# Moving the 8-bit coding of x and context from ScalarE to VectorE, and attention's row term from the front to the down stage

## The chip, the cores and the metric

The kernel runs on one NeuronCore of a Trainium2 chip. The core has TensorE (PE, matrix products into PSUM), VectorE (DVE), ScalarE (ACT), GpSimd (POOL) and SyncE (SP), which here issues nearly every DMA, in one queue and in program order. Every engine works through its own instructions in order and waits for others by semaphores. The metric is the device time of one execution in microseconds (us).

## The reference, cut to what matters

`x` is (2, 512, 1024), the context (2, 1024, 1024), both float32. The block is a quantised product with the context, then a quantised gated feed-forward layer (hidden width 2752):

```
q1 = fake_quant(layernorm(x), s1, z1)      # clip(round(v / s + z), 0, 255), minus z, times s
q2 = fake_quant(ctx, s2, z2)
x1 = x + tanh(g_xattn) * (q1 @ q2)
A  = blockwise fp8 of layernorm(x1), the last 128 columns twice (value and remainder)
h  = silu(A @ Wg.T * g) * (A @ Wu.T * g)   # Wg, Wu: blockwise int4
out = x1 + tanh(g_ffn) * (blockwise fp8 of h) @ Wd.T * gm
```

With zero points that are not whole numbers, q1 @ q2 has, beside the product of whole-number codes, a term for each column and a term for each row. The row term is one number per row of x. It cancels in the layernorm of x1, so the kernel adds it apart from the rest, to the copy of x1 that goes into the output.

## The kernel before, in words

The 1024 rows of x are 8 tiles of 128 (t = 0..7), the 2048 context rows 16 tiles (c = 0..15). Everything is written out by hand, engine by engine: the order in the source is the order on the engine, and there is no scheduler.

**Front (about 0 to 83 us).** SP loads x (`load_x`), then context tiles (`load_ctx`) into six buffers, so load c waits until code c - 6 is made (semaphore `ctx_affine`). Weight pieces for the first products (`load_piece(0)` to `(3)`) are loaded in between. Context tile c goes through `relu_ctx(c)` on ACT (scale, add the zero point, clip below at 0, write uint8 with rounding and saturation into one of two byte buffers `ctx_int`), `shift_ctx(c)` on POOL (subtract the rounded zero point, write bf16 into `ctxq`), and `col_sums` on PE. Tile t of x goes through `first_stats(t)` on DVE, `layernorm` (one call for tiles 0 to 3, one for 4 to 7), `relu_x(t)` on ACT (as for the context), `quantise_x(t)` on DVE (uint8 to bf16), `turn_x(t)` on PE (eight transposes) and `aT_out(t)` on ACT. Then PE runs `attend(t)`, and DVE's `make_x1(t)` adds the result into x. Between its first steps DVE also works out two flags (are the column permutations the identity?); SP reads them (`flags_ready`, two register loads) after `load_ctx(6)` and before `load_ctx(7)`.

**Preparation of the feed-forward layer (about 60 to 140 us).** ACT squares x1 (`square_x1`) and normalises it (`norm(t)`, `xn_done`), DVE takes block maxima (`max_a`); after all 8 tiles the maximum goes over PE (`spread_max`) and gives the global scale. From there on the activations are quantised, transposed by DMA (`turn_a`) and multiplied. In parallel, weight piece n passes DVE (`front_open`: block maxima, scales), POOL (`scale`), ACT (`round_w`, `whole_w`), POOL (`back_open`), ACT (`hi_open`), POOL (`lo_open`, `nat_lo`), and a DMA transpose (`turn_piece(n)`). `base(t)` on ACT adds the row term to x1 in place, after `norm(t)`, and SP's `store_x1(t)` puts the result to DRAM (`x1_d`). The transposed pieces 0 to 2 (`p_ring`) take the place of x1's tiles 0 to 2, so `turn_piece(0)` waits until these three tiles are stored (`x1_gone`). SP's order here is load_piece(4), store_x1(0), store_x1(1), load_piece(5), store_x1(2), turn_piece(0), load_piece(6), store_x1(3) and so on; load_piece(n) waits for lo_open(n - 4).

**Main loop and down stage (140 us to the end).** PE runs gate and up products and, from 589 us, the down products, 130 matmuls for each row tile. In the down stage ACT makes `magic_h` and `hi_h` for each half of a row tile, DVE the rest of the quantisation, SP loads x1 back (`load_x1`), and DVE's `finish(t)` adds x1 to the product before `store_out(t)`.

Of the kernel before, what the change touches and what calls it, by code (L numbers as in the profile page):

```python
# [13 lines left out]
ALU = mybir.AluOpType  # L14
ACT = mybir.ActivationFunctionType
# [51 lines left out]
def gated_block(nc, x, ctx_in, g_xattn, g_ffn, s1, z1, s2, z2, w_gate, w_up, w_down, ri_in, ri_mid, out):  # L67
# [4 lines left out]
    with ExitStack() as ctx:  # L72
# [143 lines left out]
        att_done = sem("att_done")  # L216
        x_base = sem("x_base")
        x1_ready = sem("x1_ready")
# [125 lines left out]
        def _(sp):  # L344
# [495 lines left out]
        def _(act):  # L840
# [10 lines left out]

            def relu_ctx(c):

                w = ctx_buf[c % CTX_BUFS]
                act.wait_ge(ctx_loaded[c % CTX_BUFS], 16 * (c // CTX_BUFS) + 16)
                if c >= 2:

                    act.wait_ge(ctx_quant, c - 1)
                act.activation(ctx_int[:, c % 2, :], w, ACT.Relu, bias=prm[:, 3:4], scale=pinv[:, 1:2]).then_inc(ctx_affine, 1)  # L859

            def relu_x(t):

                act.wait_ge(ln_ready, t // 4 + 1)
                if t >= 2:

                    act.wait_ge(a_quant, t - 1)
                act.activation(x_int[:, t % 2, :], x_all[:, t, :], ACT.Relu, bias=ln_add[:, t:t + 1],
                               scale=ln_mul[:, t:t + 1]).then_inc(x_affine, 1)

            def aT_out(t):  # L870
# [22 lines left out]
            def norm(t):  # L893

                if t == 0:
# [5 lines left out]
                               scale=ln_mul[:, t:t + 1]).then_inc(xn_done, 1)  # L901

            def base(t):

                act.wait_ge(row_term_ready, 1)
                act.wait_ge(xn_done, t + 1)
                act.activation(x_all[:, t, :], x_all[:, t, :], ACT.Identity, bias=row_term[:, t:t + 1]).then_inc(x_base, 1)

# [79 lines left out]
            relu_x(3)
            relu_ctx(15)
            square_x1(0)  # L990
            aT_out(2)
            square_x1(1)
            relu_x(4)
            relu_x(5)
            relu_x(6)
            aT_out(3)
# [3 lines left out]
            square_x1(2)  # L1000
            relu_x(7)
            round_w(0, 1)
# [16 lines left out]
            norm(3)  # L1019
            base(0)  # L1020
            hi_open(1)
            base(1)
            hi_open(2)
            square_x1(7)
            base(2)
            round_w(3, 0)
            root(4, slice(4, NT))
            base(3)
            whole_w(3)
            norm(4)  # L1030
            round_w(4, 1)
            base(4)
            norm(5)
            hi_open(3)
            norm(6)
            base(5)
            norm(7)
            base(6)
            round_w(5, 2)
            base(7)  # L1040
            round_w(6, 3)
# [103 lines left out]
            def hi_h(n):  # L1145
# [209 lines left out]
        def _(dve):  # L1355
# [233 lines left out]
            step(dve.tensor_tensor(tt[:, 1:2], tt[:, 0:1], fz[:, 1:2], ALU.mult))  # L1589
            dve.tensor_scalar(tt[:, 2:3], tt[:, 1:2], fz[:, 0:1], float(H), ALU.mult, ALU.mult).then_inc(prm_ready, 1)  # L1590
            step(first_stats(3))
            first_stats(4)
            first_stats(5)
            dve.wait_ge(idx_loaded, 32)
# [6 lines left out]
            dve.tensor_reduce(nfl[0:64, 1:2], neq[0:64, 8:8 + nm], AX_X, ALU.max).then_inc(flag_step, 1)  # L1601
            aggregate(slice(0, 4))
            dve.wait_ge(flag_step, 5)
            dve.tensor_reduce(nall[:, 0:1], acc[3][:, 0:2 * P], AX_X, ALU.max)
            step(dve.tensor_reduce(nall[:, 1:2], acc[3][:, P:2 * P], AX_X, ALU.max))
            dve.tensor_copy(flag[:], nall[:]).then_inc(flags_ready, 1)
            layernorm(1, slice(0, 4), tt[:, 5:6], prm[:, 1:2])
            first_stats(6)
            step(first_stats(7))
            aggregate(slice(4, NT))  # L1610
            quantise_x(0)
            dve.wait_ge(flags_ready, 1)
            in_moved = dve.value_load(flag[0:1, 0:1], min_val=0, max_val=1)
            quantise_x(1)
            col_lo(0)
            quantise_x(2)
            make_x1(0)
            layernorm(2, slice(4, NT), tt[:, 5:6], prm[:, 1:2])
            make_x1(1)
            quantise_x(3)  # L1620
            quantise_x(4)
            make_x1(2)
            quantise_x(5)
            col_lo(1)
# [256 lines left out]
```

## Time and profile before

| what | us |
|---|---|
| median of 3 runs | 818.23 (816.87 to 818.39) |
| profiled execution, its own time | 818.77 |
| its span, first to last instruction | 817.0 |
| PE busy in the span | 731.0 (89%) |
| DVE busy | 556.3 (68%) |
| POOL busy | 343.7 (42%) |
| ACT busy | 311.3 (38%) |

Outside the span lie 1.77 us of the profiled execution. Busy time is a sum over stages that have different limits, so the sections below read it stage by stage. In rows of the timeline an entry with "x2" or more is several instructions in one row, and the duration is from the first start to the last end. An instruction's duration includes time in which it has started and is held up.

### The profile page before, as it was taken

What the parts mean: (1) busy time and instruction counts of PE and PEld (TensorE: products, weight loads), DVE (VectorE), ACT (ScalarE), POOL (GpSimd) and SP (SyncE); (2) the same over time, 40 slices, a digit from 0 to 9 for tenths busy, and PEclk for the clock granted to TensorE, in tenths of its full rate; (3) what the DMA queues carried; (4) which work ended last, traced back from release to release, by engine and by line L of the source; (5) the groups of instructions that cost most, each with busy time, mean ns of one, the idle gap of its engine ahead of it and who ended that gap; (6) DMA issues with size and microseconds to landing.
All of it is one profiled execution on the core that took longest, in us unless ns stands there. A gap on an engine that the chain in (4) does not pass through costs nothing.

```text
span 817.0 us, 10350 instructions
## 1 busy us (share of the span) xinstructions
PE 731.0 (89%) x3473; PEld 334.5 (41%) x3473; DVE 556.3 (68%) x957; ACT 311.3 (38%) x382; POOL 343.7 (42%) x206
## 2 busy tenths in 40 slices
PE   0599003999999999999999999999999999999998
PEld 0144002545444444444444444444444444444443
DVE  5459789894475756675757575745898888988800
ACT  2798972445252524343434343430222122121100
POOL 1536766769374747584848575740000000000000
PEclk9989655999999999999999999999999999999999
DMA  8910598339588897979697969774265654555320
GB/s 308 353 60 14 166 279 147 80 64 190 145 173 212 187 211 174 223 169 227 145 232 163 231 163 236 157 157 164 49 152 162 182 129 149 132 161 121 88 60 26
DMA packets 228884, 131.56 MB, mean 161 GB/s; under 512 B 201712, under 2 KB 212976, under 8 KB 227824
## 3 DMA queue, kind: packets, MB, share of 16 engines
q1 hardware_dynamic: 228848, 131.12, 65.2%
q8 instruction: 18, 0.29, 0.2%
q14 instruction: 18, 0.15, 0.1%
HBM read 61.88 MB, written 19.66 MB: 100 GB/s over the span
## 4 chain that ended last, share of the span: by engine, by line
PE 78%; DVE 5%; POOL 5%; DMA 5%; ACT 3%; SPq 2%; issue 1%; DVEq 0%
PE acc L1276 47%; PE acc L1330 27%; DMA big<-in_ctx_dram 3%; PE acc L1223 2%; POOL big L739 1%; POOL h_in L734 1%; DVE big L1535 1%; ACT wbuf_all L919 1%; POOL wbuf_all L715 1%; POOL wbuf_all L708 1%; POOL big L728 1%; DMA wbuf_all<-in_L_ffn_w_up_dram 1%; SPq L455 1%; DMA mid<-big 1%; DMA x_d<-big 1%
## 5 line engine op out<-in xcount | busy, mean ns | idle before, releaser
L1276 PE MATMUL acc<-mid 128*128 128x512 f16 x1920 | 415.1, 379 | 0.0
L1276 PEld LDWEIGHTS acc<-mid 128*128 128x128 f16 x1920 | 187.9, 98 | 226.1
L1330 PE MATMUL acc<-big,mid 128*128 128x512 f16 x1040 | 224.6, 379 | 0.0
L818 POOL TENSOR_TENSOR h_in<-wbuf_all,h_in 128x1024 f16<-128x1024 f32 (+1 forms) x56 | 114.4, 2044 | 97.2 <-ACT h_in L1115 97.1
L1330 PEld LDWEIGHTS acc<-big,mid 128*128 128x128 f16 x1040 | 101.8, 98 | 122.7
L708 POOL TENSOR_TENSOR wbuf_all<-wbuf_all,w_inv 128x1024 f32<-128x1024 f32 (+1 forms) x67 | 125.2, 1873 | 43.6 <-DVE w_inv L1448 43.6
L1558 DVE SCALAR_TENSOR_TENSOR h_out<-acc,gs,silu 128x256 f32<-128x256 f32 (+1 forms) x88 | 41.5, 471 | 102.6 <-ACT silu L956 65.3
L1442 DVE TENSOR_REDUCE tb<-wbuf_all 128x64 f32<-128x1024 f32 (+1 forms) x67 | 78.9, 1178 | 47.3 <-DMA wbuf_all<-in_L_ffn_w_gate_dram 22.2
L912 ACT ACTIVATE wbuf_all<-wbuf_all 128x1024 f32<-128x1024 f32 (+1 forms) x67 | 68.1, 1016 | 82.2 <-POOL wbuf_all L708 81.4
L1115 ACT ACTIVATE h_in<-wbuf_all 128x1024 f16<-128x1024 f32 (+1 forms) x56 | 56.9, 1016 | 103.1 <-DVE wbuf_all L1454 103.1
L1454 DVE SCALAR_TENSOR_TENSOR wbuf_all<-wbuf_all,tb 128x1024 f32<-128x1024 f32 (+1 forms) x56 | 65.1, 1163 | 0.3 <-issue 0.2
L1153 ACT ACTIVATE wbuf_all<-h_in 128x1408 f16<-128x1408 f32 x16 | 22.0, 1377 | 108.4 <-DVE h_in L1509 67.9
L956 ACT ACTIVATE silu<-acc,gs 128x256 f32<-128x256 f32 (+1 forms) x88 | 40.0, 456 | 50.2 <-PE acc L1276 49.4
L1143 ACT ACTIVATE wbuf_all<-h_in 128x1408 f32<-128x1408 f32 (+1 forms) x16 | 21.6, 1351 | 50.6 <-DVE h_in L1773 50.6
L1276 PE MATMUL acc<-big,mid 128*128 128x384 f16 x192 | 34.4, 341 | 2.1 <-DMA mid<-big 1.3
L1811 DVE SCALAR_TENSOR_TENSOR mid<-acc,hr,mid 128x512 f32<-128x512 f32 x16 | 11.4, 745 | 36.2 <-PE acc L1330 36.2
L1563 DVE TENSOR_REDUCE hm<-h_out 128x256 f32 (+2 forms) x88 | 34.0, 387 | 2.7
L1783 DVE SCALAR_TENSOR_TENSOR h_in<-wbuf_all,h_in 128x1408 f32<-128x1408 f32 (+1 forms) x16 | 25.4, 1587 | 10.1 <-ACT wbuf_all L1143 10.1
L1448 DVE RECIPROCAL w_inv<-tb 128x64 f32<-128x64 f32 (+1 forms) x56 | 30.2, 539 | 1.9
L1223 PE MATMUL acc<-mid,big 128*128 128x512 bf16 x128 | 31.5, 403 | 0.0
L702 POOL TENSOR_SCALAR mid<-big,nrz 128x1024 bf16<-128x1024 uint8 x16 | 18.4, 1151 | 30.4 <-ACT big L859 30.1
L1773 DVE SCALAR_TENSOR_TENSOR h_in<-mid,hr,h_in 128x1408 f32<-128x1408 f32 (+1 forms) x16 | 26.3, 1646 | 0.3
(159 smaller groups left out, 555.0 us busy)
## 6 DMA issues: line engine op xcount, KB each, us to landing
h_in<-h_d SPq DMA_DIRECT2D x8, 1376.0 KB, 7.0
wbuf_all<-in_L_ffn_w_gate_dram SPq DMA_DIRECT2D x21, 512.0 KB, 4.3
wbuf_all<-in_L_ffn_w_up_dram SPq DMA_DIRECT2D x21, 512.0 KB, 4.3
h_d<-h_out SPq DMA_DIRECT2D x80, 128.0 KB, 3.5
big<-in_ctx_dram SPq DMA_DIRECT2D x16, 512.0 KB, 10.7
wbuf_all<-in_L_ffn_w_down_dram SPq DMA_DIRECT2D x16, 512.0 KB, 4.5
big<-in_x_dram SPq DMA_DIRECT2D x8, 512.0 KB, 6.9
x_d<-big SPq DMA_DIRECT2D x8, 512.0 KB, 4.8
```

Of the source, the lines that this page charges most:

```text
L708: pool.tensor_tensor(w, w, spread(w_inv[0:rows, b, 0:cols // BLK]), ALU.mult).then_inc(w_scaled, 1)
L818: last = pool.tensor_tensor(nat[s % 4][:, H:H + cols], wbuf[:, s % 4, 0:cols], nat[s % 4][:, 0:cols], ALU.subtract)
L912: act.activation(wbuf[0:rows, b, 0:cols], wbuf[0:rows, b, 0:cols], ACT.Copy, bias=MAGIC, scale=W_UP)\
L956: act.activation(silu[:, m % 2, 0:cols], acc[m % 4][:, 0:cols], ACT.Silu, scale=gs[:, 2:3]).then_inc(silu_done, 1)
L1115: act.activation(nat[s % 4][:, 0:cols], wbuf[:, s % 4, 0:cols], ACT.Copy).then_inc(nat_hi, 1)
L1223: pe.matmul(acc[pair(t) + hf][:], aT[:, k, t * P:(t + 1) * P], ctxq[:, b * KT + k, hf * MW:(hf + 1) * MW], start=(k == 0), stop=False)
L1276: last = pe.matmul(acc[m % 4][:, 0:cols], left[:, k, s * P:(s + 1) * P], w[:, right, k, 0:cols], start=(k == 0 and left is a_hi and right ...
L1330: last = pe.matmul(acc[2 * i + hf][:], left[:, k - ks.start, :], right[:, k, hf * MW:(hf + 1) * MW], start=(k == 0 and left is hi and righ ...
L1442: dve.tensor_reduce(top, blocks(wbuf[0:rows, b, 0:cols]), AX_X, ALU.max, apply_absolute_value=True).then_inc(scale_step, 1)
L1454: dve.scalar_tensor_tensor(out=w, in0=w, scalar=MAGIC, in1=spread(block_scale(b, looped)[0:rows, 0:cols // BLK]), op0=ALU.subtract, op1=AL ...
L1558: dve.scalar_tensor_tensor(out=h_out[:, m % 2, 0:cols], in0=acc[m % 4][:, cols:2 * cols], scalar=gs[:, 2:3], in1=silu[:, m % 2, 0:cols], o ...
L1563: dve.tensor_reduce(hm[:, s, bass.ds(at, cols // BLK)], blocks(h_out[:, m % 2, 0:cols]), AX_X, ALU.max, apply_absolute_value=True).then_in ...
```

## The change

Coding of x and context is done on DVE by new functions `code_ctx` and `code_x`: one two-step tensor_scalar (multiply, add) from float32 to uint8, without the Relu, since the conversion saturates at 0. They stand in DVE's program among the first steps. ACT's 16 `relu_ctx` and 8 `relu_x` are gone, and so are its 8 `base` calls in the preparation. SP stores x1 as soon as `make_x1(t)` has made it. `turn_piece(0)` now also waits for the first three `norm` calls, which read what it overwrites. In the down stage ACT adds the row term to the x1 tile that was loaded back, in place, and `finish(t)` waits for that (`x1_based`) in place of the load.

```
+                        sp.wait_ge(xn_done, X1_FIRST)          # in turn_piece(0)
...
             def store_x1(t):
-                sp.wait_ge(x_base, t + 1)
+                sp.wait_ge(x1_ready, t + 1)
...
+            def base(t):                                       # ACT, down stage
+                i = t % 2
+                act.wait_ge(x1_loaded[i], 16 * (t // 2 + 1))
+                act.activation(x1_t[:, i, :], x1_t[:, i, :], ACT.Identity, bias=row_term[:, t:t + 1]).then_inc(x1_based, 1)
...
             magic_h(4)
+            base(0)
             for n in range(4, 2 * NT):
                 hi_h(n)
                 if n + 1 < 2 * NT:
                     magic_h(n + 1)
+                    if n % 2 == 1:
+                        base((n - 3) // 2)
+            base(NT - 2)
+            base(NT - 1)
...
+            def code_ctx(c):                                   # DVE
+                dve.wait_ge(ctx_loaded[c % CTX_BUFS], 16 * (c // CTX_BUFS) + 16)
+                if c >= 2:
+                    dve.wait_ge(ctx_quant, c - 1)
+                dve.tensor_scalar(ctx_int[:, c % 2, :], ctx_buf[c % CTX_BUFS], pinv[:, 1:2], prm[:, 3:4], ALU.mult, ALU.add)\
+                    .then_inc(ctx_affine, 1)
+            def code_x(t):
+                if t % 4 == 0:
+                    dve.wait_ge(ln_ready, t // 4 + 1)
+                dve.tensor_scalar(x_int[:, t % 2, :], x_all[:, t, :], ln_mul[:, t:t + 1], ln_add[:, t:t + 1], ALU.mult, ALU.add)\
+                    .then_inc(x_affine, 1)
...
             def finish(t):
-                dve.wait_ge(x1_loaded[i], 16 * (t // 2 + 1))
+                dve.wait_ge(x1_based, t + 1)
```

DVE's program from the parameters on is now: code_ctx(0), stats(3), code_ctx(1), first half of the flags, aggregate(0..3), code_ctx(2), second half of the flags, code_ctx(3), layernorm(1), code_ctx(4), code_x(0), stats(4), code_ctx(5), quantise_x(0), stats(5), code_ctx(6), stats(6), code_ctx(7), code_x(1), stats(7), code_ctx(8), quantise_x(1), aggregate(4..7), code_ctx(9), code_x(2), code_ctx(10), quantise_x(2), col_lo(0), code_ctx(11), code_x(3), layernorm(2), code_ctx(12), quantise_x(3), make_x1(0), code_ctx(13), code_x(4), code_ctx(14), quantise_x(4), code_ctx(15), make_x1(1), code_x(5), code_x(6), make_x1(2), quantise_x(5), col_lo(1), front_open(0), quantise_x(6), code_x(7), make_x1(3), and from there as before.

**DVE around the flags.** These rows of DVE's program run from the statistics of x's tile 3 to the end of the flag work; nfl, nall and flag are the flags, mv and ve the variance of tiles 0 to 3. Before:

```order
L1367 BN_STATS bst<-big 128x6 x6
L1597 TENSOR_TENSOR neq<-idx,iot 128x8
L1598 TENSOR_TENSOR neq<-idx,iot 64x43
L1600 TENSOR_REDUCE nfl<-neq 128x1
L1601 TENSOR_REDUCE nfl<-neq 64x1
L1372 BN_AGGR mv<-bst 128x2 x4
L1374 TENSOR_SCALAR ve<-mv 128x4
L1604 TENSOR_REDUCE nall<-acc3 128x1
L1605 TENSOR_REDUCE nall<-acc3 128x1
L1606 CAST flag<-nall 128x2
```

And these are the rows of the changed program, from the same point on (rows `big<-big,pinv,prm` are code_ctx(0), (1) and (2)):

```order
L1364 TENSOR_SCALAR big<-big,pinv,prm 128x1024
L1324 BN_STATS bst<-big 128x6 x2
L1364 TENSOR_SCALAR big<-big,pinv,prm 128x1024
L1570 TENSOR_TENSOR neq<-idx,iot 128x8
L1571 TENSOR_TENSOR neq<-idx,iot 64x43
L1573 TENSOR_REDUCE nfl<-neq 128x1
L1574 TENSOR_REDUCE nfl<-neq 64x1
L1329 BN_AGGR mv<-bst 128x2 x4
L1331 TENSOR_SCALAR ve<-mv 128x4
L1364 TENSOR_SCALAR big<-big,pinv,prm 128x1024
L1578 TENSOR_REDUCE nall<-acc3 128x1
L1579 TENSOR_REDUCE nall<-acc3 128x1
```

The last flag step (CAST) is the next row. Three codes of the context now stand ahead of it, the first of them ahead of everything.

**DVE at the first weight piece.** The rows go from the first weight piece's maxima and scales (front_open(0), w_max and w_inv) over quantise_x(6) to make_x1(3). Before:

```order
L1442 TENSOR_REDUCE tb3<-wbuf_all 128x64
L1445 TENSOR_SCALAR w_max<-tb3 128x64
L1448 RECIPROCAL w_inv<-w_max 128x64
L1407 TENSOR_SCALAR silu<-big,nrz 128x1024
L1414 SCALAR_TENSOR_TENSOR big,x_sum<-acc0,tt,big 128x512
L1414 SCALAR_TENSOR_TENSOR big,x_sum<-acc1,tt,big 128x512
```

And the same place of the changed program:

```order
L1415 TENSOR_REDUCE tb3<-wbuf_all 128x64
L1418 TENSOR_SCALAR w_max<-tb3 128x64
L1421 RECIPROCAL w_inv<-w_max 128x64
L1380 TENSOR_SCALAR silu<-big,nrz 128x1024
L1371 TENSOR_SCALAR big<-big,ln_mul,ln_add 128x1024
L1387 SCALAR_TENSOR_TENSOR big,x_sum<-acc0,tt,big 128x512
L1387 SCALAR_TENSOR_TENSOR big,x_sum<-acc1,tt,big 128x512
```

One row is new, code_x(7), between quantise_x(6) and make_x1(3).

**ACT in the preparation.** The rows go from norm(3) (`big<-big,ln_add,ln_mul`) to square_x1(7) (`hm,x_sq`) and the next round_w; `h_in<-wbuf_all` is hi_open(1) and (2). Before:

```order
L900 ACTIVATE big<-big,ln_add,ln_mul 128x1024
L907 ACTIVATE big<-big,row_term 128x1024
L928 ACTIVATE h_in<-wbuf_all 128x1024
L907 ACTIVATE big<-big,row_term 128x1024
L928 ACTIVATE h_in<-wbuf_all 128x1024
L890 ACTIVATE hm,x_sq<-big,n_mean 128x1024
L907 ACTIVATE big<-big,row_term 128x1024
L912 ACTIVATE wbuf_all<-wbuf_all 128x1024
```

And of the changed program:

```order
L883 ACTIVATE big<-big,ln_add,ln_mul 128x1024
L905 ACTIVATE h_in<-wbuf_all 128x1024 x2
L873 ACTIVATE hm,x_sq<-big,n_mean 128x1024
L889 ACTIVATE wbuf_all<-wbuf_all 128x1024
L851 ACTIVATE sq<-ve 128x4
```

The three base calls (`big<-big,row_term`) are gone from this place, and nothing else moved.

## Rows read from the trace of the kernel before

**Rows 1.** Stretches: length; busy PE, PEld, DVE, ACT, POOL; clock; DMA share; GB/s.

```profile
42.00:43.00 1.00, 1.00 (x3) 0.30 (x2) 1.00 (x2) 1.00 (x2) 0.00 (x0) 0.50 1.01 401
60.00:80.00 20.00, 20.00 (x161) 9.42 (x159) 18.82 (x38) 17.07 (x23) 11.24 (x6) 1.00 0.00 1
80.00:100.00 20.00, 3.02 (x14) 1.02 (x12) 16.19 (x30) 19.63 (x23) 15.08 (x8) 0.65 0.57 159
```

**Rows 2.** Chain that ended last, start and duration in us, near 26 to 40 us.

```profile
26.17 10.50 DMA big<-in_ctx_dram
...
36.70 1.25 ACT big L859
...
39.20 1.03 PE tb L1208 x2
```

**Rows 3.** The same chain, near 90 to 103 us.

```profile
90.21 1.05 ACT big L907
91.27 4.19 DMA x_d<-big
...
97.52 5.53 DMA wbuf_all<-in_L_ffn_w_up_dram
```

**Rows 4.** ACT's coding of the context, 18 to 42 us: count, busy, mean, idle before.

```profile
L859 ACT ACTIVATE big<-big,prm,pinv 128x1024 uint8<-128x1024 f32 x11 | 13.5, 1236 | 11.3 <-DMA big<-in_ctx_dram 11.1
```

**Rows 5.** Timeline of ACT: its first codes of the context, and the wait before.

```profile
18.74 3.79 ACT L859 ACTIVATE big<-big,prm,pinv 128x1024 uint8<-128x1024 f32 x3 [6.16 <-DMA big<-in_ctx_dram]
```

**Rows 6.** Timeline of DVE, 18 to 31 us: start, duration, line, operation, operands.

```profile
18.09 0.17 DVE L1606 CAST flag<-nall 128x2 int32<-128x2 f32 x1
...
25.21 1.10 DVE L1394 TENSOR_SCALAR ln_add<-rstd,prm 128x4 f32<-128x4 f32 x1
26.22 2.46 DVE L1367 BATCH_NORM_STATS2 bst<-big 128x6 f32<-128x512 f32 x4
29.86 0.74 DVE L1407 TENSOR_SCALAR silu<-big,nrz 128x1024 bf16<-128x1024 uint8 x1
```

**Rows 7.** Timeline of POOL at the same time and near 70 us.

```profile
25.17 1.12 POOL L702 TENSOR_SCALAR mid<-big,nrz 128x1024 bf16<-128x1024 uint8 x1 [0.20 <-ACT big L859]
...
69.95 2.46 POOL L715 TENSOR_TENSOR wbuf_all<-wbuf_all,w_max 128x1024 f32<-128x1024 f32 x1
```

**Rows 8.** Timeline of SP: the loads of context tiles 6 and 7.

```profile
20.01 0.34 SPq L354 DMA_DIRECT2D big<-in_ctx_dram  x1
...
22.50 0.35 SPq L354 DMA_DIRECT2D big<-in_ctx_dram  x1
```

**Rows 9.** DMA issues, 79 to 88 us: count, size, median us to landing.

```profile
wbuf_all<-in_L_ffn_w_gate_dram SPq DMA_DIRECT2D x1, 512.0 KB, 3.2
```

**Rows 10.** Timeline of PE: products of attend(0) and attend(1).

```profile
40.03 6.17 PE L1223 MATMUL acc<-mid,big 128*128 128x512 bf16 x16
47.12 3.62 PE L1223 MATMUL acc<-mid,big 128*128 128x512 bf16 x16
```

**Rows 11.** Timeline of DVE, 58 to 73 us.

```profile
58.74 0.74 DVE L1407 TENSOR_SCALAR h_out<-big,nrz 128x1024 bf16<-128x1024 uint8 x1
60.32 1.41 DVE L1426 SCALAR_TENSOR_TENSOR big<-tb,tt,big 1x512 f16<-1x512 f32 x2 [0.84 <-ACT big L880]
...
63.75 0.65 DVE L1407 TENSOR_SCALAR silu<-big,nrz 128x1024 bf16<-128x1024 uint8 x1
...
68.28 0.75 DVE L1414 SCALAR_TENSOR_TENSOR big<-acc,tt,big 128x512 f32<-128x512 f32 x1 [0.30 <-PE acc L1228]
70.53 1.90 DVE L1379 TENSOR_SCALAR ve<-x_sq 128x4 f32<-128x4 f32 x1
```

**Rows 12.** Timeline of POOL, the first scale of a weight piece.

```profile
63.92 2.28 POOL L708 TENSOR_TENSOR wbuf_all<-wbuf_all,w_inv 128x1024 f32<-128x1024 f32 x1 [11.95 <-DVE w_inv L1448]
```

**Rows 13.** Timeline of SP: load_piece(5).

```profile
90.53 0.33 SPq L412 DMA_DIRECT2D wbuf_all<-in_L_ffn_w_up_dram  x1
```

**Rows 14.** Timeline of ACT in the down stage: hi_h of row tile 3.

```profile
653.37 1.38 ACT L1153 ACTIVATE wbuf_all<-h_in 128x1408 f16<-128x1408 f32 x1 [5.01 <-DVE h_in L1785]
```

More of the change, by code:

```diff
@@ L216, in gated_block @@
         att_done = sem("att_done")
-        x_base = sem("x_base")
+        x1_based = sem("x1_based")
         x1_ready = sem("x1_ready")
@@ L850, in root @@
                 act.activation(sq[:, ts], ve[:, ts], ACT.Sqrt).then_inc(sqrt_done, 1)
[L852 to L868, printed above, removed]
             def aT_out(t):
@@ L901, in norm @@
                                scale=ln_mul[:, t:t + 1]).then_inc(xn_done, 1)
[L903 to L907, printed above, removed]
             def round_w(n, b, rows=P, cols=H):
@@ L992, in _ @@
             square_x1(1)
-            relu_x(4)
-            relu_x(5)
-            relu_x(6)
             aT_out(3)
@@ L1000, in _ @@
             square_x1(2)
-            relu_x(7)
             round_w(0, 1)
@@ L1019, in _ @@
             norm(3)
-            base(0)
             hi_open(1)
-            base(1)
             hi_open(2)
             square_x1(7)
-            base(2)
             round_w(3, 0)
             root(4, slice(4, NT))
-            base(3)
             whole_w(3)
@@ L1031, in _ @@
             round_w(4, 1)
-            base(4)
             norm(5)
@@ L1035, in _ @@
             norm(6)
-            base(5)
             norm(7)
-            base(6)
             round_w(5, 2)
-            base(7)
             round_w(6, 3)
@@ L1153, in hi_h @@
                 act.activation(nat_part(0, ks), h_in[:, t % 2, ks.start * P:ks.stop * P], ACT.Copy).then_inc(nat_h_hi, 1)
+            def base(t):
+                i = t % 2
+                act.wait_ge(x1_loaded[i], 16 * (t // 2 + 1))
+                act.activation(x1_t[:, i, :], x1_t[:, i, :], ACT.Identity, bias=row_term[:, t:t + 1]).then_inc(x1_based, 1)
+            act.wait_ge(row_term_ready, 1)
             silu_unit(UNITS_D, 0)
@@ L1590, in _ @@
             dve.tensor_scalar(tt[:, 2:3], tt[:, 1:2], fz[:, 0:1], float(H), ALU.mult, ALU.mult).then_inc(prm_ready, 1)
+            code_ctx(0)
             step(first_stats(3))
-            first_stats(4)
-            first_stats(5)
+            code_ctx(1)
             dve.wait_ge(idx_loaded, 32)
@@ L1602, in _ @@
             aggregate(slice(0, 4))
+            code_ctx(2)
             dve.wait_ge(flag_step, 5)
@@ L1606, in _ @@
             dve.tensor_copy(flag[:], nall[:]).then_inc(flags_ready, 1)
+            code_ctx(3)
             layernorm(1, slice(0, 4), tt[:, 5:6], prm[:, 1:2])
+            code_ctx(4)
+            code_x(0)
+            first_stats(4)
+            code_ctx(5)
+            quantise_x(0)
+            first_stats(5)
+            code_ctx(6)
             first_stats(6)
+            code_ctx(7)
+            code_x(1)
             step(first_stats(7))
+            code_ctx(8)
+            quantise_x(1)
             aggregate(slice(4, NT))
-            quantise_x(0)
+            code_ctx(9)
             dve.wait_ge(flags_ready, 1)
             in_moved = dve.value_load(flag[0:1, 0:1], min_val=0, max_val=1)
-            quantise_x(1)
+            code_x(2)
+            code_ctx(10)
+            quantise_x(2)
             col_lo(0)
-            quantise_x(2)
-            make_x1(0)
-            layernorm(2, slice(4, NT), tt[:, 5:6], prm[:, 1:2])
+            code_ctx(11)
+            code_x(3)
+            layernorm(2, slice(4, NT), tt[:, 5:6], prm[:, 1:2])
+            code_ctx(12)
+            quantise_x(3)
+            make_x1(0)
+            code_ctx(13)
+            code_x(4)
+            code_ctx(14)
+            quantise_x(4)
+            code_ctx(15)
             make_x1(1)
-            quantise_x(3)
-            quantise_x(4)
+            code_x(5)
+            code_x(6)
             make_x1(2)
@@ L1626, in _ @@
             quantise_x(6)
+            code_x(7)
             make_x1(3)
```

20 lines of the change are left out of this document (removed).

## The prediction, made before the changed kernel was run

> **What bounds the kernel now.** I read the stretches first, then the chain that ended last, then the timelines of the engines that the change touches. From 140 us on PE is full, so what can be won or lost is the time at which PE starts on the feed-forward products. Ahead of that, PE does almost nothing from 83 us on; between 80 and 100 us ACT is busy 19.63 of 20 us, and between 60 and 80 us DVE 18.82 and PE 20.00 [rows 1]. Busy is not bound, so the chain decides. It has two stretches that matter here. Context tile 9 lands at 36.67 us, after 10.50 us in the DMA queue; ACT codes it, POOL shifts it, and PE goes on at 39.20 [rows 2]. Later, the store of x1's tile 2 starts at 91.27 and takes 4.19 us, turn_piece(0) follows when it has landed, load_piece(6) at 97.52, and its 5.53 us end at 103.05; DVE has waited for that weight piece before it can finish the maxima that give the global scale [rows 3]. So the front is bound by DMA arrivals and then by one in-order queue, SP.
>
> **ACT gets lighter, and nothing waits for it.** A code costs ACT 1236 ns [rows 4], about 1.14 from start to start, so 24 of them are some 27 us that leave ACT; eight base calls of 1.05 us [rows 3] are 8.4 more. What hides this gain: the codes are made as fast as the tiles land (11.1 us of ACT's idle time ahead of these codes are waits for the DMA [rows 4]). As for base: store_x1(2) stands behind load_piece(5) in SP, which was issued at 90.53, when POOL had made lo_open(1) [rows 13]. Without base the store goes out right behind it, at about 91.03 and not at 91.27. The gain is 0.25 us, no more.
>
> **DVE gets 24 codes.** No row shows float32 to uint8 on DVE. The nearest is quantise_x, uint8 to bf16, same length and kind: 0.74 us alone, 0.65 behind another [rows 6, 11]. The bounds are 0.65 and, if it ran at one element a cycle as the statistics do (2.46 us for 4 x 512, so 1.23 for 1024 [rows 6]), 1.25. I take 0.65 to 0.74.
>
> These operations also block one another with POOL. DVE's ln_add, a tensor_scalar of 4 elements, takes 1.10 us from 25.21 and ends at 26.31, with POOL's shift running from 25.17 to 26.29 [rows 6, 7]. The same at 70.53: 1.90 us for 4 elements, to 72.43, and POOL's back_open ends at 72.41 [rows 7, 11]. The statistics, beside POOL's work too, keep their 0.62 per call [rows 6]. When both wait, they take turns: back_open, issued at 69.95, was stretched to 2.46 us by the quantise_x ahead of it, and went ahead of the next DVE operation. So each POOL shift (1.12 us [rows 7]) holds the next code, and each code holds the shift.
>
> The Trainium skill, page "SBUF — State Buffer", section "SBUF: two separate sides", says that DVE and GpSimd share one pair of ports as an exclusive lock, held for the whole instruction, against DVE operations in a two-port mode or with two SBUF inputs. The trace agrees, with the 1.10 and 1.90 us above. By that rule ACT's codes never blocked anybody and DVE's will, so it speaks against this change; without it the same sum would be that of the first rival below.
>
> **Step 1, the flags and the seventh load.** Tile 0 of the context lands at 18.7 us [rows 5]. DVE now waits for it with statistics of tile 3 and the flags behind. From 18.75: code 0.65, statistics 1.3, code 0.7, flag half 0.5, aggregate 0.4, a 4-element tensor_scalar that waits for POOL's shift (to 22.9), code 0.7, maxima 0.7, and the CAST, which waits for the next shift: flags at about 25.0, not 18.26 [rows 6]. SP took from 20.35 to 22.50 between load_ctx(6) and load_ctx(7), with the flags already there, so about 2.1 us are its own [rows 8]. Load 7 goes out at about 27.1, when tile 6 has landed and the queue is empty. A lone load takes 3.2 us [rows 9], so it lands at 30.3. Tile 9 took 14.2 us from load 7's issue (22.50 to 36.67), part of it backlog; without backlog I put it at 39, between 37 and 40.
>
> **Step 2, DVE up to code 9.** From 25.05: codes 3 to 8, code_x(0) and (1), quantise_x(0) and (1) are 10 x 0.65 = 6.5; layernorm 1.2 plus one wait for POOL 1.0; statistics 4 x 1.25 = 5.0; aggregate 0.6 plus a wait of 0.8. Sum 15.1, so DVE reaches code 9 at about 40.2. Both steps agree. Shift and PE follow as before (36.70 to 39.20 was 2.50 with ACT's 1.25; with 0.7 it is 2.0): PE goes on at 42.3, 3.1 us late.
>
> **Step 3, to the first weight piece.** From 40.3 to the end of quantise_x(5), DVE has fourteen codes and quantisings (9.2), column part and layernorm (2.8), three make_x1 of 1.6 (4.8): 16.8. Waits for POOL: code_x(2), layernorm, code 14 and code 15 at 1.1 each, and 1.3 in smaller ones: 5.7. It ends at 62.8; before it was 58.74 + 0.75 = 59.49 [rows 11]. Between here and front_open(0) DVE stood idle 0.84 us for ACT's column part [rows 11]; that takes up as much, and 2.5 of the 3.3 us are left. DVE binds here rather than PE, since attend(0) may even be faster, see below.
>
> **Step 4, code_x(7).** quantise_x(6) starts at 63.75, POOL's scale was issued at 63.92 and took 2.28 [rows 11, 12]: it gets the port when quantise_x(6) ends, at about 64.4, and keeps it to 66.2. code_x(7) now stands there and waits 1.9, then runs 0.7: make_x1(3), which followed quantise_x(6) at once, is 2.6 us later. It needed no wait for POOL; one of its two inputs is in PSUM. Of DVE's later idle time only 0.30 could absorb this [rows 11], and PE is late too. Slip 2.5 + 2.6 = 5.1 us, and from here DVE is dense to front_open(4), which releases lo_open(1), so load_piece(5), store_x1(2), turn_piece(0) and load_piece(6) follow it.
>
> **Step 5, the down stage.** Eight base calls of about 1.1 us on ACT, behind magic_h of an even half. ACT stands idle 5.01 us at exactly that place [rows 14], the x1 tile was loaded a row tile earlier, and finish(t) comes about 4 us later. Cost 0; if that cover were gone, up to 1.1 us a tile, 8.8.
>
> **Sum.** 5.1 - 0.25 = 4.9 us later at the global scale, and everything behind it keeps its distance. 818.77 + 4.9 = 823.7 for the profiled execution; it lies 0.54 over the median, so 823.1 against the median of 818.23.
>
> **Rivals.**
> (a) The port costs little: DVE and POOL slide into each other's gaps. Then flags 23.9, load 7 lands at 29.2, tile 9 at 38.3, PE 1.2 late, code_x(7) 0.35 net: 1.2 + 0.35 - 0.25 = 1.3, 819.5. For it: in the front POOL is idle most of the time. Against: shifts follow codes at once, so that they meet by construction.
> (b) Faster, by PE's clock. The granted clock stood at 0.50 (1.2 GHz) in attend(0) [rows 1], ahead of which PE had waited for tile 9 until 39.20 [rows 2]; its 16 matmuls took 6.17 us where attend(1)'s took 3.62 [rows 10]. If the steadier arrival of codes leaves no such gap, 2.6 us come back. With tile 9 and DVE as in (a): 1.3 - 2.6 = -1.3, and with tile 9 no later than before -2.5: 815.7 to 816.9. It decides only if DVE reaches quantise_x(5) before PE does; its own work, 16.8 us from 41, says 58, with no wait at all. The Trainium skill, "TensorE: Matmul & The Clock Gate", section "HAM oscillation — how this bites in real kernels", says that gaps in PE's work send it back to half clock; the rows agree (6.17 against 3.62).
> (c) The code runs at one element a cycle: 24 x 0.55 = 13 us more on DVE, of which some 12 lie before quantise_x(5), less the waits for the port (1.8 and 5.7 us in steps 2 and 3), since such an operation may not need it, and less 1.9 + 0.5 net in step 4: 823.1 + 12 - 7.5 - 1.4 = 826.2.
> (d) base in the down stage delays hi_h: 8.8 us at most, 827 to 832. Against it stand 5.01 us of idle time.
>
> **Chances.** Forecast 0.55, (a) 0.18, (b) 0.12, (c) 0.11, (d) 0.04. A difference under 0.2% (1.6 us, 816.6 to 819.9) is about what a measurement of this kernel can't tell from no change; most of (a) and a little of (b) and the forecast fall there, in all 0.15. Faster 0.11, slower 0.74. The forecast's own range is 821 to 825.5 (steps 2 to 4 by 2 us either way); the range given, with (a) and most of (c), is 818 to 826.5.
>
> **What would show it.** Step 1: SP's load of tile 7 at 27 us, the CAST at 25. Step 2: PE's matmuls on tile 9 near 42. Mean of the codes: 0.7 to 0.8 if free, over 1 where POOL runs; uniformly 1.25 is (c). Step 4: code_x(7) of about 2.5 us. Base: store_x1(2) right behind load_piece(5), at 96; the part from there to PE's first product unchanged. Step 5: hi_h in the down stage with 5.01 - 1.1 = 3.9 us idle before it, and PE full there as before. I am wrong if the DVE timeline shows 4-element operations without waits, or if load_piece(6) comes at 98 or before.

## The result, and the profile after

The changed kernel takes 823.89 us (median of 4 runs, 823.71 to 824.22) against 817.55 us for the kernel before on the same chip (4 runs, 816.86 to 818.39): ratio 1.0077, 95% interval 1.0061 to 1.0093. It is slower, by 6.3 us; 823.1 was forecast, within the range.

The profiled span is 821.9 us, 4.9 longer than before. One thing has to be taken off before two timelines are compared: the DMA brought the first context tile at another moment in each execution. The first code began at 18.74 us before [rows 5] and at 17.73 after. Counted from there the slip is 1.0 us more, some 5.9 in the span. Times below that are called "from the first code" are counted in this way.

The chain that ended last in the changed kernel (start and duration in us, what) takes the same two stretches as [rows 2, 3], later:

```profile
29.54 10.68 DMA big<-in_ctx_dram
40.25 0.82 DVE big L1364
41.16 1.13 POOL mid L703
42.33 1.03 PE tb L1165 x2
...
66.97 2.34 DVE big L1371
...
95.90 5.12 DMA x_d<-big
101.04 1.89 SPq L456
...
103.08 5.28 DMA wbuf_all<-in_L_ffn_w_up_dram
```

Lines have moved: L1364 is the context's code on DVE, L1371 x's code, L456 turn_piece, L703 POOL's shift. The new link is the one at 66.97: x's code held for 2.34 us.

The flag work in DVE's timeline (start, duration, line, operation, operands), which was done at 18.26 before [rows 6]:

```profile
17.73 0.81 DVE L1364 TENSOR_SCALAR big<-big,pinv,prm 128x1024 uint8<-128x1024 f32 x1 [6.14 <-DMA big<-in_ctx_dram]
...
21.43 0.40 DVE L1331 TENSOR_SCALAR ve<-mv 128x4 f32<-128x4 f32 x1
21.73 0.80 DVE L1364 TENSOR_SCALAR big<-big,pinv,prm 128x1024 uint8<-128x1024 f32 x1
...
23.09 0.67 DVE L1580 CAST flag<-nall 128x2 int32<-128x2 f32 x1
23.67 0.80 DVE L1364 TENSOR_SCALAR big<-big,pinv,prm 128x1024 uint8<-128x1024 f32 x1
...
25.01 0.69 DVE L1346 SCALAR_TENSOR_TENSOR ln_mul<-rstd,tt,sq 128x4 f32<-128x4 f32 x1
```

A free code takes 0.79 to 0.81 us from issue to end and 0.73 from start to start. The CAST of two elements takes 0.67 us where it took 0.17 [rows 6]: it ends with POOL's shift, which runs from 22.62 to 23.74. SP issues context load 7 2.1 us after it, and POOL's rows show what the codes do to the shifts:

```profile
25.88 0.35 SPq L354 DMA_DIRECT2D big<-in_ctx_dram  x1
```

```profile
22.62 1.12 POOL L703 TENSOR_SCALAR mid<-big,nrz 128x1024 bf16<-128x1024 uint8 x1 [0.82 <-DVE big L1364]
...
26.97 1.62 POOL L703 TENSOR_SCALAR mid<-big,nrz 128x1024 bf16<-128x1024 uint8 x1 [1.28 <-DVE big L1364]
29.60 1.55 POOL L703 TENSOR_SCALAR mid<-big,nrz 128x1024 bf16<-128x1024 uint8 x1 [1.02 <-DVE big L1364]
...
41.16 1.12 POOL L703 TENSOR_SCALAR mid<-big,nrz 128x1024 bf16<-128x1024 uint8 x1 [2.75 <-DVE big L1364]
...
66.48 2.27 POOL L709 TENSOR_TENSOR wbuf_all<-wbuf_all,w_inv 128x1024 f32<-128x1024 f32 x1 [7.75 <-DVE w_inv L1421]
```

Groups between 16 and 68 us (count, busy, mean ns, idle before): the shift's mean is 1382 ns, and was 1151 in the same stretch before.

```profile
L1364 DVE TENSOR_SCALAR big<-big,pinv,prm 128x1024 uint8<-128x1024 f32 x16 | 14.5, 907 | 8.1 <-DMA big<-in_ctx_dram 8.0
L1371 DVE TENSOR_SCALAR big<-big,ln_mul,ln_add 128x1024 uint8<-128x1024 f32 x8 | 8.8, 1110 | 0.1
```

DVE at code 9, and from quantise_x(5) to make_x1(3), which answers to [rows 11]:

```profile
40.25 0.81 DVE L1364 TENSOR_SCALAR big<-big,pinv,prm 128x1024 uint8<-128x1024 f32 x1 [1.82 <-DMA big<-in_ctx_dram]
```

```profile
62.05 0.74 DVE L1380 TENSOR_SCALAR h_out<-big,nrz 128x1024 bf16<-128x1024 uint8 x1
62.89 1.40 DVE L1399 SCALAR_TENSOR_TENSOR big<-tb,tt,big 1x512 f16<-1x512 f32 x2
...
66.32 0.66 DVE L1380 TENSOR_SCALAR silu<-big,nrz 128x1024 bf16<-128x1024 uint8 x1
66.89 2.42 DVE L1371 TENSOR_SCALAR big<-big,ln_mul,ln_add 128x1024 uint8<-128x1024 f32 x1
69.23 0.74 DVE L1387 SCALAR_TENSOR_TENSOR big<-acc,tt,big 128x512 f32<-128x512 f32 x1
```

code_x(7), in 66.89 to 69.31, is held by POOL's scale (66.48 to 68.75) and ends 0.56 us behind it. The 0.84 us for which DVE stood at the column part in [rows 11] are gone: there is no idle time ahead of 62.89.

SP, where load_piece(5), store_x1(2), the turning and load_piece(6) follow one another:

```profile
95.36 0.33 SPq L412 DMA_DIRECT2D wbuf_all<-in_L_ffn_w_up_dram  x1
95.90 0.33 SPq L490 DMA_DIRECT2D x_d<-big  x1
101.04 1.89 SPq L456 DMA_TRANSPOSE big<-h_in  x1
103.08 1.05 SPq L412 DMA_DIRECT2D wbuf_all<-in_L_ffn_w_up_dram  x1
```

Step by step, in us from the first code. "Flags" is the end of their CAST, "maxima" the start of PE's turning of the column maxima for the global scale, before and after:

```profile
109.62 0.47 PE L1183 MATMUL tb<-ident,gmx 128*128 128x128 f32 x1 [26.61 <-DVE gmx L1655]
```

```profile
114.93 0.47 PE L1140 MATMUL tb<-ident,gmx 128*128 128x128 f32 x1 [27.86 <-DVE gmx L1652]
```

| event | before | after | slip | slip forecast |
|---|---|---|---|---|
| flags | -0.5 | 6.0 | 6.5 | 6.7 |
| context load 7 issued | 3.8 | 8.2 | 4.4 | 4.6 |
| PE goes on with tile 9 | 20.5 | 24.6 | 4.1 | 3.1 |
| quantise_x(5) ends | 40.7 | 45.1 | 4.3 | 3.3 |
| make_x1(3) starts | 45.6 | 51.5 | 5.9 | 5.1 |
| load_piece(5) issued | 71.8 | 77.6 | 5.8 | 5.1 |
| store_x1(2) issued | 72.5 | 78.2 | 5.6 | 4.9 |
| load_piece(6) issued | 78.8 | 85.4 | 6.6 | 4.9 |
| maxima | 90.9 | 97.2 | 6.3 | 4.9 |

The last slip equals the 6.3 us by which the medians differ, but in these two traces the span counted in this way is 5.9 longer. PE's next matmul follows the maxima by 25.8 us in both. About 0.3 us come back near 202 us: PE waited 0.32 us there for a DMA before the change, and does not after it. In the down stage hi_h of the row tile of [rows 14] reads

```profile
658.30 1.38 ACT L1098 ACTIVATE wbuf_all<-h_in 128x1408 f16<-128x1408 f32 x1 [3.97 <-DVE h_in L1782]
```

with 3.97 us idle before it instead of 5.01: the row term's 1.04 us came out of that idle time.

### The profile page after: what moved, and what is told of

It reads as the page before. It is cut to its first block, busy times and chain, and to the rows that moved or that the text cites. A ratio compares the mean times of both kernels' runs of the same rounds, so it can differ in the third digit from the quotient of the medians.

```text
span 821.9 us, 10336 instructions
## 1 busy us (share of the span) xinstructions
PE 730.7 (89%) x3473; PEld 334.4 (41%) x3473; DVE 576.7 (70%) x981; ACT 284.2 (35%) x358; POOL 347.5 (42%) x206
## 4 chain that ended last, share of the span: by engine, by line
PE 79%; DVE 9%; POOL 4%; DMA 4%; issue 1%; SPq 1%; ACT 1%; DVEq 0%
PE acc L1233 49%; PE acc L1287 27%; DMA big<-in_ctx_dram 2%; PE acc L1180 1%; POOL h_in L735 1%; POOL big L729 1%; DVE big L1508 1%; DVE tb L1415 1%; DVE h_in L1433 1%; POOL big L740 1%; DMA wbuf_all<-in_L_ffn_w_up_dram 1%; DVE big L1387 1%; DMA x_d<-big 1%; SPq L347 1%; DVE big L1364 1%
## 5 line engine op out<-in xcount | busy, mean ns | idle before, releaser
L703 POOL TENSOR_SCALAR mid<-big,nrz 128x1024 bf16<-128x1024 uint8 x16 | 22.1, 1382 | 33.4 <-DVE big L1364 33.4
## 6 DMA issues: line engine op xcount, KB each, us to landing
big<-in_ctx_dram SPq DMA_DIRECT2D x16, 512.0 KB, 10.7
```

## The experiments

Each ran beside the kernel before on the same chip, but the experiments were spread over three chips. The ratio is to the kernel before. A difference to the changed kernel, or between two experiments, is my subtraction of medians; where the ratios give another figure, both stand.

| kernel | median us | ratio, 95% interval |
|---|---|---|
| changed kernel | 823.89 | 1.0077 (1.0061 to 1.0093) |
| flag work first | 821.32 | 1.0043 (1.0027 to 1.0060) |
| code_x(7) early | 821.74 | 1.0049 (1.0030 to 1.0068) |
| both | 819.65 | 1.0032 (1.0021 to 1.0044) |
| shifts on ACT | 823.49 | 1.0067 (1.0054 to 1.0080) |
| all three | 818.63 | 1.0010 (0.9999 to 1.0020) |
| codes on DVE, base as before | 822.98 | 1.0067 (1.0048 to 1.0085) |
| before, base in the down stage | 817.47 | 1.0004 (0.9992 to 1.0015) |
| changed, load_piece(6) first | 819.29 | 1.0017 (1.0008 to 1.0026) |
| all three and load_piece(6) first | 813.6 | 0.9946 (0.9930 to 0.9961) |
| before, load_piece(6) first | 813.82 | 0.9957 (0.9942 to 0.9972) |
| that, and base in the down stage | 812.3 | 0.9933 (0.9917 to 0.9948) |

**Which half of the change costs.** Two kernels split it. In the first the codes are on DVE and the row term is added in the front, by base(0) to base(7) in ACT's program as before:

```diff
-                sp.wait_ge(x1_ready, t + 1)
+                sp.wait_ge(x_base, t + 1)
...
+            base(0)
...
-                dve.wait_ge(x1_based, t + 1)
+                dve.wait_ge(x1_loaded[i], 16 * (t // 2 + 1))
```

> The changed kernel, with only the row term put back: base on ACT in the preparation, none in the down stage; the codes stay on DVE. Theory A (base is hidden in both places): 0 to 0.5 us slower than the changed kernel, 824.1 us, store_x1(2) at 96.0 to 96.3 in place of 95.90. Rival (the eight base calls were a load on the path, 8.4 us of ACT's time): 2 to 8 us slower than the changed kernel, 826 to 832. Second rival (base in the down stage costs): up to 2 us faster.

The second is the kernel before with the row term alone moved (the same lines the other way).

> The kernel before, with only the row term moved to the down stage; the codes stay on ACT. Theory A: 0.25 us faster than before, which can't be told from no change, 817.3 us; store_x1(2) right behind load_piece(5), near 91.0 in place of 91.27; ACT's idle time before hi_h of a full row tile in the down stage 3.9 in place of 5.0 us. Rival (relief of ACT where it was 98% busy pays): 2 us faster or more, 815.5.

They took 822.98 and 817.47 us. So the codes bring the loss, and the row term's move alone is worth nothing that these runs can tell from no change. The first one's 0.9 us under the changed kernel is within the two intervals (1.0048 to 1.0085 and 1.0061 to 1.0093), but the traces say where such a difference can sit. With base in the front the store of tile 2 goes out 0.74 us behind load_piece(5) and has landed after 4.2 us (before) and 4.5 (here); in the seven kernels without it and with the old order of SP it goes out 0.55 us behind and takes 4.65 to 5.14. Counted from load_piece(5), it lands after 4.95 and 5.25 us with base in the front, and after 5.20 to 5.68 without: it goes out earlier and lands no earlier. That the two transfers share the DMA engines would explain this; no run here isolates it.

**Step 1: the flags.** The flag work is put ahead of the first code:

```diff
-            code_ctx(0)
             step(first_stats(3))
-            code_ctx(1)
...
             aggregate(slice(0, 4))
-            code_ctx(2)
...
             dve.tensor_copy(flag[:], nall[:]).then_inc(flags_ready, 1)
+            code_ctx(0)
+            code_ctx(1)
+            code_ctx(2)
             code_ctx(3)
```

> The changed kernel, with DVE's statistics of tile 3 and the whole flag work put back ahead of code_ctx(0). Theory A (the flags hold SP's load of context tile 7, and that load's landing holds everything up to PE's first attention product): load 7 goes out at about 22.5 us in place of 25.88, tile 9 lands near 36.7 to 37.5 in place of 40.25, PE goes on near 39 in place of 42.33, and all that follows is 3 to 3.5 us earlier: 820.5 us, ratio to the kernel before 1.0035. Theory B (DVE's own work and its waits for POOL bind as much, and the late load is a second thing of the same size): DVE reaches code 9 later than tile 9 lands, and less than 1.5 us comes back: 822.5 or more.

It took 821.32 us, 2.6 less than the changed kernel. SP goes on to the context loads as early as before (load 8 at 22.48 us), the ninth tile is there when DVE comes to it, and the wait of 1.82 us for the DMA is gone:

```profile
22.56 1.53 DVE L1364 TENSOR_SCALAR big<-big,pinv,prm 128x1024 uint8<-128x1024 f32 x1 [1.09 <-POOL mid L703]
...
37.94 0.80 DVE L1364 TENSOR_SCALAR big<-big,pinv,prm 128x1024 uint8<-128x1024 f32 x1
```

But DVE's own work now brings it to code 9 only at 19.85 us from the first code (before, on ACT: 17.96). The load was late by 4.4 us and that cost 2.6; what is left of the lateness at code 9 (1.9 us) is DVE's, its work and its waits for POOL.

**Step 4: x's last code.** It is moved ahead of the piece's opening, where POOL has nothing to do (with a wait for quantise_x, whose buffer it writes):

```diff
             col_lo(1)
+            dve.wait_ge(a_quant, 6)
+            code_x(7)
             front_open(0)
             quantise_x(6)
-            code_x(7)
             make_x1(3)
```

> The changed kernel, with code_x(7) moved from behind quantise_x(6) to ahead of front_open(0), where POOL has nothing to do. Theory A (code_x(7) costs what it waits for POOL's scale): it takes 0.8 us in place of 2.42, make_x1(3) starts near 67.7 in place of 69.23, and 1.3 to 1.6 us come back: 822.4 us. Rival (the chain behind it is bound by something else, such as PE or POOL, and the wait was covered): within 0.4 us of the changed kernel, 823.5 to 824.2.

821.74 us, 2.2 less than the changed kernel. The code takes its free 0.81 us, make_x1(3) follows quantise_x(6) at once, and a part of the gain is lost to PE (the 0.39 us below):

```profile
65.22 0.81 DVE L1371 TENSOR_SCALAR big<-big,ln_mul,ln_add 128x1024 uint8<-128x1024 f32 x1
...
67.93 0.65 DVE L1380 TENSOR_SCALAR silu<-big,nrz 128x1024 bf16<-128x1024 uint8 x1
68.50 0.74 DVE L1387 SCALAR_TENSOR_TENSOR big<-acc,tt,big 128x512 f32<-128x512 f32 x1
...
72.55 0.75 DVE L1387 SCALAR_TENSOR_TENSOR big<-acc,tt,big 128x512 f32<-128x512 f32 x1 [0.39 <-PE acc L1185]
...
74.14 2.47 DVE L1380 TENSOR_SCALAR h_out<-big,nrz 128x1024 bf16<-128x1024 uint8 x1
```

quantise_x(7) took 1.15 us at this place in the changed kernel and 2.47 here, but the 4-element operation behind it, held for 1.90 there, takes 0.16 here. The pair takes 2.5 us and not 2.9, so the wait for POOL changed its row and did not grow. This profiled execution took 823.05 us, 1.3 over the median of its kernel, and its maxima come 1.2 us earlier than the changed kernel's: it shows the cause, but only a part of the 2.2 us.

**Do the shifts on POOL matter?** They are given to ACT, which the change had freed, among its calls of root, aT_out, col_out and square_x1:

```diff
+            def shift_ctx(c):
+                act.wait_ge(ctx_affine, c + 1)
+                act.activation(ctxq[:, c, :], ctx_int[:, c % 2, :], ACT.Identity, bias=nrz[:, 1:2]).then_inc(ctx_quant, 1)
...
+            shift_ctx(0)
+            shift_ctx(1)
             root(1, slice(0, 4))
+            shift_ctx(2)
```

> The changed kernel, with the 16 shifts of the context (uint8 to bf16) moved from POOL to ACT, so that POOL runs nothing beside DVE's codes until the first weight piece's scale at 66 us. Theory A (DVE's codes and POOL's shifts hold one another): DVE's codes all take 0.8 us, the 1.6 us ones at 41, 54 and 56 us are gone, the 4-element operations at 21.4, 37.8 and 47.4 take 0.2; load 7 goes out 0.5 to 0.8 us earlier, quantise_x(5) ends 1.5 to 2.5 us earlier, code_x(7) keeps its 2.4; 821.7 us. Rival (the long codes have another cause, such as SBUF traffic by the DMA): durations stay, and the time is within 0.5 us of the changed kernel's 823.9.

823.49 us: 0.4 less (0.8 by the ratios), which can't be told from nothing. Yet the holding up is gone: the sixteen codes take 809 ns each and not 907, and the 4-element operations their 0.2.

```profile
L1369 DVE TENSOR_SCALAR big<-big,pinv,prm 128x1024 uint8<-128x1024 f32 x16 | 12.9, 809 | 10.0 <-DMA big<-in_ctx_dram 9.9
```

What took its place stands in DVE's timeline of this kernel:

```profile
40.54 0.81 DVE L1369 TENSOR_SCALAR big<-big,pinv,prm 128x1024 uint8<-128x1024 f32 x1 [2.75 <-DMA big<-in_ctx_dram]
...
60.40 0.75 DVE L1392 SCALAR_TENSOR_TENSOR big<-acc,tt,big 128x512 f32<-128x512 f32 x1 [1.93 <-PE acc L1190]
...
63.58 1.40 DVE L1404 SCALAR_TENSOR_TENSOR big<-tb,tt,big 1x512 f16<-1x512 f32 x2 [0.84 <-ACT big L852]
```

The flags are DVE's own work for the most part and come only 0.7 us sooner (5.3 from the first code). So DVE reaches code 9 sooner, but its wait for the tile grows from 1.82 to 2.75 us; then DVE waits 1.93 us for PE, whose attend(2) had waited 1.34 us for a copy that ACT now makes behind two shifts; then 0.84 for ACT's column part, as before the change. The column part starts at 44.9 us from the first code, and did at 45.2 without this edit. And code_x(7) is still held for 2.42 us by the scale. So my expectation, which took the stretched codes as time on the path, fell: the lock shows everywhere in this stretch, and the load, PE and ACT were late behind it. But 0.4 us is a net figure. The edit takes the lock away and puts sixteen shifts of 1.14 us on ACT: at make_x1(2) DVE was ready 2.9 us earlier than in the changed kernel before it waited those 1.93 us. No run takes the lock alone away.

All three edits together, and the first two without the shifts:

> The changed kernel with three repairs together: flags ahead of code_ctx(0), code_x(7) ahead of front_open(0), shifts on ACT. Theory A (flags and load 7, code_x(7), and the waits for POOL are separate terms that add up to what the change lost): 2.6 + 1.6 + 2.0 us come back, 817.6 us, equal to the kernel before. Rival (the terms overlap, since PE's attention with its slow first product sets the end of this stretch): 819.5 us.

> The changed kernel with the flag work first and the seventh code of x early, the shifts still on GpSimd (with the shifts on ScalarE as well it took 818.6 us; the two edits alone gave 2.6 and 2.2 us). Theory A: the lock of the shared port between the codes and the shifts is worth little on the path, once the seventh context load is not late and x's code is out of the scale's way: the two edits add up, 823.9 - 4.7 = 819.2 us, and the shifts are worth 0.6 us. Rival B: with the load early, the context pass is bound by VectorE, and there the lock counts (some eight codes 0.8 us longer each, of which the path sees two to three): 820.5 us or more.

818.63 and 819.65 us. Flags and code are worth 4.2 together (2.6 + 2.2 alone, so nearly additive: they cover different stretches); by the ratios it is 3.7. With them done the shifts on ACT are worth 1.0, or 1.8 by the ratios (the two kernels ran on different chips), while they were worth 0.4 alone. The theories gave 0.6 and 1.9, and these runs don't decide between them. In the kernel with the first two edits the context's codes take 1033 ns each, with 1.0 us of idle time for POOL; with all three 809. Of the 6.3 us these edits take back 5.3; what is left, ratio 1.0010, can't be told from no change.

**The queue behind the store.** In [rows 3] load_piece(6) stands behind turn_piece(0), and that behind the landing of store_x1(2), though the load needs neither. Here it goes first:

```diff
             store_x1(2)
-            turn_piece(0)
             load_piece(6)
+            turn_piece(0)
```

In the changed kernel:

> The changed kernel, with SP's load_piece(6) ahead of turn_piece(0) in place of behind it. Theory A (the preparation is bound by this one load, which waits in SP's queue for the store of x1's tile 2): load_piece(6) goes out near 97.5 us in place of 103.08, the global maximum is done 4 to 5 us earlier and the end follows: 819.4 us. Rival (it is bound by norm(7) on ACT or by the DMA anyway, so that the load has slack): under 1 us.

819.29 us, 4.6 less. SP in this kernel:

```profile
94.71 0.33 SPq L412 DMA_DIRECT2D wbuf_all<-in_L_ffn_w_up_dram  x1
95.25 0.33 SPq L490 DMA_DIRECT2D x_d<-big  x1
96.79 0.33 SPq L412 DMA_DIRECT2D wbuf_all<-in_L_ffn_w_up_dram  x1
100.05 1.82 SPq L456 DMA_TRANSPOSE big<-h_in  x1
```

The load goes out 2.1 us behind load_piece(5) and not 7.7, and the chain runs through the load before it (94.71, 4.08 us) instead. The maxima are 7.0 us earlier, counted from the first code, and PE's next matmul some 6, but the span is only 4.5 shorter: the rest was not followed up. In the kernel before, and with all three earlier edits:

> The kernel before, with load_piece(6) ahead of turn_piece(0). Theory A: load_piece(6) goes out near 92.6 us in place of 97.5, and then norm(7), which stands behind base calls in ACT, is next to bind (103.2 us): 4.0 to 4.7 us faster than before, 813.2. Rival: under 1 us.

> The changed kernel with all four edits: flag work first, the seventh code of x in the gap ahead of the piece's opening, the shifts on ScalarE, and the load of piece 6 ahead of the first turning (without the last edit: 818.6 us; the last edit alone gave 4.6 us). Theory A: the edits cover different stretches (25 to 62, 62 to 75 and 95 to 103 us) and add up: 818.6 - 4.6 = 814.0 us, the same as the kernel before with the early load (813.8). Rival B: the early load binds only after other work has been late, so part of it is gone with the others: 815.5 us or more.

813.82 and 813.6 us. The edit is worth 4.0 us on the kernel before (3.5 by the ratio) and 5.0 on the other (5.2). With all four edits the changed kernel stands level with the kernel before plus the one. That is not yet a verdict on the codes, since the first of the two also has the row term in the down stage.

Last, the row term again. With load 6 early ACT has no idle time in its queue from 91.1 to 104.7 us, and three of the eight base calls stand in it among the norms that the maxima need. So on this ground the move to the down stage should pay:

> The kernel before with both the row term moved to the down stage and the load of weight piece 6 ahead of the first piece's turning (the kernel before with the moved load alone took 813.8 us). With the load early, ScalarE is busy without a gap from 91.1 to 104.7 us, with three row-term additions (1.04 us each) among norms that the column maxima wait for. Theory A: what comes last is then VectorE's own chain of column maxima; with the additions gone (the changed kernel with the early load has none) the stretch from rstd's square root to the maxima's matmul is 11.7 us in place of 12.4: 0.8 us less, 813.0 us. Rival B: ScalarE's queue is the bound, all three additions come off it: 811.8 us or less. Rival C: nothing, 813.8 us or more.

812.3 us, ratio 0.9933; the fastest kernel of this study, 1.5 us under the same without the move, with intervals that overlap at 0.9942 to 0.9948. It differs from the 813.6 us kernel by the codes and the edits made for them: with the row term in the down stage in both, and load 6 early in both, the codes on DVE are 1.3 us behind (ratios 0.9946 and 0.9933), which again is inside the intervals. The traces show where the row term's 1.5 us can sit. ACT with base in the front (first fence) and without (second):

```profile
93.22 1.22 ACT L900 ACTIVATE big<-big,ln_add,ln_mul 128x1024 f32<-128x1024 f32 x1
...
95.30 1.13 ACT L907 ACTIVATE big<-big,row_term 128x1024 f32<-128x1024 f32 x1
...
99.55 1.13 ACT L907 ACTIVATE big<-big,row_term 128x1024 f32<-128x1024 f32 x1
100.59 1.23 ACT L900 ACTIVATE big<-big,ln_add,ln_mul 128x1024 f32<-128x1024 f32 x1
```

```profile
92.92 1.24 ACT L901 ACTIVATE big<-big,ln_add,ln_mul 128x1024 f32<-128x1024 f32 x1
...
97.09 2.36 ACT L901 ACTIVATE big<-big,ln_add,ln_mul 128x1024 f32<-128x1024 f32 x2
```

From ACT's square root (91.12 and 91.69) to PE's turning of the maxima (103.56 and 103.30) it is 12.4 us with base and 11.6 without: the 0.8 expected. The rest came behind it: from there to PE's next matmul 27.7 and 26.7 us, since with base ACT was still at work that its additions had pushed back when the scaling of h should start (DVE waits 1.41 us for it at 107.12). None of my theories had that second part.

## Why the prediction was right

The direction and the order of the links were right, and so was the mechanism of the two that count: the late flags and the held code_x(7), undone together, give back 4.2 of the 6.3 us. The sum was 1.4 us short (4.9 forecast, 6.3 measured): 0.7 of it lies ahead of load_piece(5), in step 1, and 0.7 behind it, in the store. One further step came out right by luck.

Step 1 held: flags 6.0 us from the first code (6.3 forecast), load 7 at 8.2 (8.4). The size that failed is "without backlog I put it at 39": tile 9 came at 40.25, 22.5 from the first code, not 20.3. From load 7's issue to the tile it took 14.4 us, as long as before (14.2), although the queue had run empty (the DMA share was 0.00 from 25 to 26 us, and 0.91 before the change). Load 7 itself gained from that, 3.9 us to landing for 5.0. Load 9 did not: it goes out 3.7 us behind load 7 in both kernels (26.17 and 29.54), behind load 7, load 8 and four loads of weight pieces, and takes 10.5 and 10.7 us from then on. In this time there is a stretch in which the DMA engines are busy throughout but move few bytes, 226 GB/s from 29 to 34 us before and 229 from 30 to 37 after. It is 2 us longer, and why is open. In step 2 DVE was ready at 38.42, 20.7 from the first code, 0.8 sooner than my sum. The two errors point opposite ways, and the later arrival decides: PE's slip is 1.0 us larger than forecast.

Step 3's total is right: 22.5 us from 40.25 to the end of quantise_x(5), as forecast. But two errors cancel in it, and that is luck. The program has sixteen codes and quantisings there, not fourteen, and a free code costs 0.73 us from start to start, not 0.65: DVE's own work was 18.8 us for my 16.8. The waits for POOL were 3.7 for my 5.7: code 14 and 15 were held 0.8 us each, code_x(2) 1.1 with the gap ahead of it, the layernorm 0.7. The slip of 4.3 has that 1.0 of step 2 in it, and 3.6 were left at the column part, after the 0.84 of idle time. That 24 codes at one element a cycle would have cost 1.25 each is excluded by the 0.81.

Step 4: code_x(7) was held as described, 2.42 us for 2.5, and the slip grew by 2.3 us (2.6 forecast); undoing it alone gave 2.2.

Base's gain of 0.25 us did not come. The store did go out as said, at 0.55 behind the load, but took 0.9 longer to land. From load_piece(5) to the maxima the slip grew by 0.5 us where the sum let it shrink by 0.25, so this term was off by 0.7. Undone alone it has the other sign, if any (0.9 us by medians, inside the intervals).

Step 5 held exactly (3.97 us of idle time for 3.9).

By the Trainium skill's page "SBUF — State Buffer", section "SBUF: two separate sides", DVE and GpSimd share a pair of ports, and an operation of one of them locks it for its whole length. The trace agrees, with the shifts at 1.55 to 1.65 us for 1.12 and the codes at up to 2.42 for 0.81. How much of the holding between codes and shifts was on the path is not settled: the shifts on ACT gave a net 0.4 us at first, and 1.0 to 1.8 once the other waits were gone.

Rival (a), 819.5, fails as a sum. Counted from the first code it had the flags at 5.2 us and tile 9 at 19.6, and they came at 6.0 and 22.5; it had code_x(7) at 0.35, and that cost 2.3. Its premise, that the lock costs little, is wrong for the scale; for the shifts it is not settled. Rival (b) fails: in attend(0), for which [rows 1] shows a granted clock of 0.50, it was 1.00 after the change, and yet the matmuls took 5.61 us for 6.17, so only 0.56 of the 2.6 came back. DVE's rows show no wait from code 9 to front_open(0), so PE did not bind there.

```profile
43.00:44.00 1.00, 1.00 (x3) 0.30 (x2) 1.00 (x2) 0.00 (x0) 0.28 (x1) 1.00 1.03 410
```

(c) is excluded by the codes' duration, (d) by the 3.97 us of idle time that were left in the down stage.

## What to carry to other kernels

Before work is moved to an engine, look at what small thing stands behind the place where it lands: here a flag of two elements, which another queue's loads waited for, cost 2.6 of the 6.3 us. A wait that shows in every row of a stretch need not be on the path; undo it and read what is late next. A total that fits can hide two errors that cancel: compare own work and waits one by one. And look for a load that stands in a queue behind an instruction that waits for something else: here one exchanged line gave 3.5 to 4.0 us, more than any other edit, and only on top of it did taking work off ACT seem to pay.

## What the runs showed of the hardware

A row "granted clock 1.00" did not mean here that matmuls ran as fast as they could. In the changed kernel attend(0) took 5.61 us for 16 matmuls, with the clock at 1.00 from 40 to 50 us, where attend(1) took 3.62:

```profile
43.16 5.61 PE L1180 MATMUL acc<-mid,big 128*128 128x512 bf16 x16
...
49.68 3.62 PE L1180 MATMUL acc<-mid,big 128*128 128x512 bf16 x16
```

PE passed 3 to 4 matmuls a microsecond until 47 us and 6 from then on. The DMA engines were full until 47 (share 0.97 to 1.05) and nearly idle after it (0.31, then 0.04), but before the change matmuls were as slow (4 in a microsecond) from 44 to 45 us with a DMA share of 0.14, at a clock of 0.50. Which of the two, or a slow start behind PE's idle time that the clock's column does not show, is left open.

Executions of nearly equal duration differ in their first microseconds: the first code of the context began between 17.55 and 18.74 us in the thirteen traces. A difference of two spans near 1 us is not to be read without that number.
